# Router columns appended to the expert matrix, taken in pieces of 384, 384 and 264 columns; GpSimd gates the third piece

## The reference, cut to what matters

```python
# layer 0, per batch (8), 128 channels, 2304 pixels
x = x + L0_conv_ref(_gn(x), ...)          # group norm, q/k/v, softmax(q k) v, squeeze-excite
# layer 1, on tokens
t = _to_tokens(x)                          # [8, 2304, 128]
t = t + _L1_attn_ref(_ln_t(t))             # softmax(seq seq^T) seq
t = t + _L1_ffn_ref(_ln_t(t), router_w, router_b, expert_w, expert_b)

def _L1_ffn_ref(x, router_w, router_b, expert_w, expert_b):
    router_probs = softmax(x @ router_w + router_b)        # 8 experts
    top_p, top_i = top_k(router_probs, 2)
    top_p = top_p / sum(top_p)
    expert_out = einsum('bnd,edc->bnec', x, expert_w) + expert_b
    return sum over the 2 chosen experts of top_p * expert_out
```

## Time and profile before

| | |
|---|---|
| Median of 3 runs | 2558.91 us (2558.0 to 2559.78) |
| The profiled execution | 2557.83 us, of which the span of the records is 2556.1 us |
| PE busy | 2501.6 us (98%) |
| PEld busy | 2297.1 us (90%) |
| DVE busy | 2125.3 us (83%) |
| ACT busy | 1774.6 us (69%) |
| POOL busy | 544.6 us (21%) |
| granted TensorE clock | 0.998 of full speed |

### The profile page before, as it was taken

The page is one execution under the profiler, slowest core; times in us unless marked ns, Lnnn a source line. Parts: engine busy times, 40 slices in busy tenths (PEclk is TensorE's granted clock), DMA queues, the critical chain, the costliest instruction groups (busy, mean ns, idle before and its releaser), DMA issues.

```text
span 2556.1 us, 45049 instructions
## 1 busy us (share of the span) xinstructions
PE 2501.6 (98%) x14929; PEld 2297.1 (90%) x14929; DVE 2125.3 (83%) x6242; ACT 1774.6 (69%) x3478; POOL 544.6 (21%) x930
## 2 busy tenths in 40 slices
PE   7999999999999999999999999999999999999998
PEld 5889989899898998999989999899998999989997
DVE  6896888878888788887888878888789887898778
ACT  4667766677667776776767767667676677767775
POOL 0010221112220132111321113111141202312134
PEclk9999999999999999999999999999999999999999
DMA  1000000000000000000000000000000000000000
GB/s 68 10 1 1 4 29 1 23 4 7 26 1 23 4 7 26 23 1 4 10 23 23 1 4 10 23 23 1 4 10 23 23 1 4 23 10 4 1 10 13
DMA packets 13621, 32.53 MB, mean 13 GB/s; under 512 B 1616, under 2 KB 8016, under 8 KB 13392
## 3 DMA queue, kind: packets, MB, share of 16 engines
q1 hardware_dynamic: 13392, 29.64, 3.4%
HBM read 20.20 MB, written 9.44 MB: 12 GB/s over the span
## 4 chain that ended last, share of the span: by engine, by line
PE 74%; DVE 17%; ACT 5%; issue 3%; POOL 0%; DMA 0%; ACTq 0%; DVEq 0%; SPq 0%; POOLq 0%
PE ps L1239 22%; PE ps L1241 21%; PE ps L1240 21%; PE ps L1259 9%; DVE pt_lo L1040 5%; DVE row_space L1025 4%; PE ps L1386 1%; ACT row_space L775 1%; DVE pt_lo L1120 1%; ACT pt_hi L786 1%; ACT row_space L827 1%; DVE pt_lo L1125 1%; DVE gn_raw L898 1%; ACT row_space L872 0%; DVE r L1131 0%
## 5 line engine op out<-in xcount | busy, mean ns | idle before, releaser
L786 ACT ACTIVATE pt_hi<-ps 128x384 fp32r<-128x384 f32 x864 | 415.6, 488 | 301.0 <-PE ps L1259 300.7
L1040 DVE TENSOR_TENSOR pt_lo<-ps,pt_hi 128x384 fp32r<-128x384 f32 x864 | 472.6, 551 | 114.2 <-ACT pt_hi L786 112.2
L1025 DVE TENSOR_SCALAR_CACHE_REDUCE row_space<-ps,key_bias 128x512 f32<-128x512 f32 (+1 forms) x720 | 492.0, 689 | 49.0 <-PE ps L1241 48.1
L775 ACT ACTIVATE row_space<-row_space,negmax 128x512 f32<-128x512 f32 (+2 forms) x432 | 402.8, 932 | 86.0 <-DVE negmax L1034 85.2
L1259 PE MATMUL ps<-ident,row_space 128*128 128x128 f32 x2736 | 444.5, 273 | 5.0 <-ACT row_space L775 3.9
L1259 PEld LDWEIGHTS ps<-ident,row_space 128*128 128x128 f32 x2736 | 345.6, 141 | 76.1 <-ACT row_space L775 7.0
L1239 PE MATMUL ps<-pt_hi,v_hi 128*128 128x384 f32 x864 | 352.4, 408 | 17.2 <-DVE pt_lo L1040 14.9
L827 ACT ACTIVATE row_space<-ps,shift 128x768 f32<-128x768 f32 x260 | 234.1, 900 | 137.4 <-PE ps L1241 132.9
L1125 DVE TENSOR_TENSOR pt_lo<-row_space,pt_hi 128x768 fp32r<-128x768 f32 x260 | 251.3, 967 | 91.6 <-ACT pt_hi L836 91.0
L1239 PE MATMUL ps<-pt_hi,tn_hi 128*128 128x384 f32 x864 | 303.5, 351 | 2.2 <-DVE pt_lo L1125 1.1
L1241 PE MATMUL ps<-pt_hi,v_lo 128*128 128x384 f32 x864 | 292.9, 339 | 0.0
(11 more groups left out here) (229 smaller groups left out, 5396.6 us busy)
## 6 DMA issues: line engine op xcount, KB each, us to landing
x_chan<-x SPq DMA_DIRECT2D x24, 384.0 KB, 4.2
y<-acc SPq DMA_DIRECT2D x48, 192.0 KB, 1.8
t_tok<-tokens SPq DMA_DIRECT2D x8, 768.0 KB, 4.3
t_tok<-tokens SPq DMA_DIRECT2D x8, 384.0 KB, 3.1
t_tok<-eb SPq DMA_DIRECT2D x1, 516.0 KB, 5.4
t_tok<-ew SPq DMA_DIRECT2D x1, 516.0 KB, 6.7
row_space<-wqkv SPq DMA_DIRECT2D x1, 192.0 KB, 3.3
se_sb<-se SPq DMA_DIRECT2D x1, 68.0 KB, 4.1
```

Of the source, the lines that this page charges most:

```text
L775: act.activation(part, part, ACT.Exp, bias=negmax[:, r:r + 1], accum_out=dparts[:, n, r, u:u + 1]).then_inc(p_rows_ready, 1)
L786: act.activation(pt_hi[:, slot, :], ring_bank(step)[:, 0:BW], ACT.Copy)\
L1025: dve.tensor_scalar(row_part(n, r, a, w), ring_bank(step)[:, 0:w], key_bias[:, row:row + 1], None, ALU.add, ALU.max, accum_out=mx[:, row % ...
L1040: dve.tensor_tensor(pt_lo[:, slot, :], ring_bank(step)[:, 0:BW], pt_hi[:, slot, :], ALU.subtract).then_inc(pt_lo_ready, 1)
```

## The change

The 8 router columns join the 1024 expert columns in one matrix of 1032 (`ew_hi`, `ew_lo`). A tile takes it in three pieces. `expert`: 384 columns, experts 0 to 2, gated by VectorE. `scaled`: 384 columns, experts 3 to 5, gated by ScalarE. The new step `mix`: 264 columns, experts 6 and 7 and the logits. The separate router matmuls and the sum of their halves are gone. `mix` comes first for all three tiles of a block; ScalarE copies the 8 logits and then, ungated, the 256 expert columns into SBUF. `router` is VectorE's work alone and waits for the logits of the third tile. GpSimd multiplies the 256 columns by their gates and adds them up with ScalarE's terms in wider additions. `mix` and `router` join `SOON`, so that in the second attention they stand ahead of `p1low`. Most MoE slots are set anew; block 4, the left-over block, has its router no longer in stage 1 but in stage 3 of the next first attention.

```diff
-EARLIER_BLOCK = {1: {8: [('uln',)], 10: [('uapply',)], 13: [('ut',)], 16: [('router',)]}, 2: {1: [('gates',)]},
-                 3: {6: [('expert', 0)], 9: [('scaled', 0)], 12: [('expert', 1)], 13: [('scaled', 1)]},
-                 4: {4: [('expert', 2)], 9: [('scaled', 2)]}}
+EARLIER_BLOCK = {1: {8: [('uln',)], 10: [('uapply',)], 13: [('ut',)]},
+                 3: {3: [('mix', 0)], 4: [('mix', 1)], 5: [('mix', 2), ('router',)], 7: [('gates',)], 10: [('expert', 0)], 13: [('scaled', 0)]},
+                 4: {3: [('expert', 1)], 5: [('scaled', 1)], 8: [('expert', 2)], 10: [('scaled', 2)]}}
...
-MOE_SLOTS = [(6, 9, 11, [13, 13, 15, 16, 17, 18]), (22, 25, 26, [28, 28, 31, 31, 32, 33]), (31, 34, 35,
-             [37, 38, 39, 40, 41, 42]), (39, 42, 43, [45, 45, 46, 46, 47, 47]), (44, 48, 49, [50, 51, 51, 52, 52, 54])]
+MOE_SLOTS = [(6, 9, [10, 11, 11], [13, 13, 15, 16, 17, 18]), (22, 24, [25, 26, 26], [28, 28, 31, 31, 32, 33]),
+             (31, 34, [35, 35, 36], [38, 38, 39, 40, 41, 42]), (39, 42, [43, 43, 44], [46, 46, 47, 48, 49, 49]),
+             (44, 49, [50, 50, 51], [52, 53, 53, 54, 54, 55])]
...
-LAST_MOE_SLOTS = [(6, 9, 11, [13, 13, 15, 16, 17, 18]), (21, 24, 25, [26, 26, 28, 29, 30, 31]), (27, 32, 33,
...
+LAST_MOE_SLOTS = [(6, 9, [10, 11, 11], [13, 13, 15, 16, 17, 18]), (21, 24, [25, 25, 26], [28, 28, 29, 30, 31, 31]),
+                  (27, 32, [33, 33, 34], [35, 36, 36, 37, 38, 39]), (39, 41, [42, 42, 43], [44, 44, 45, 45, 46, 46]),
+                  (43, 47, [48, 48, 49], [50, 50, 51, 51, 52, 52]), (49, 53, [54, 54, 55], [57, 57, 58, 60, 60, 62]),
+                  (56, 59, [60, 61, 61], [63, 63, 64, 64, 65, 65])]
...
-SOON = ("expert", "scaled", "vproj", "qproj", "score", "row_max", "gates")
+SOON = ("mix", "router", "expert", "scaled", "vproj", "qproj", "score", "row_max", "gates")
...
+                elif kind == "mix":
+                    m, k = step[2:]
+                    act.wait_ge(ring_full, filled(step))
+                    if k == 0 and at(gates_ready, "gates", b, m) > 1:
+                        act.wait_ge(gates_ready, at(gates_ready, "gates", b, m) - 1)
+                    act.activation(logits[:, k, :], ring_bank(step)[:, 256:256 + E], ACT.Copy).then_inc(logits_ready, 1)
+                    if mix_block_before(b, m):
+                        act.wait_ge(tile_added, at(tile_added, "scaled", *mix_block_before(b, m), k))
+                    act.activation(mix_pair(m, k), ring_bank(step)[:, 0:256], ACT.Copy).then_inc(mix_terms_ready, 1)
...
                 elif kind == "router":
-                    dve.wait_ge(ring_full, filled(step))
                     shape = [128, TPB, E]
-                    link(dve.tensor_reduce(logits[:, :, :],
-                                           ring_bank(step)[:, 0:TPB * 2 * E].rearrange("p (t h e) -> p t e h", h=2,
-                                                                                       e=E), AX.X, ALU.add))
+                    dve.wait_ge(logits_ready, at(logits_ready, "mix", b, m, TPB - 1))
...
-                elif kind == "router":
-                    for k in range(TPB):
-                        pe.matmul(out, u_low(b, m)[:, tile], rw_pair[:, :, :], start=True, stop=False)
-                        ins = pe.matmul(out, u_high(b, m)[:, tile], rw_pair[:, :, :], start=False, stop=True)
+                elif kind == "mix":
+                    cols = slice(2 * GATED * 128, FOLD)
+                    three(ring_bank(step)[:, 0:256 + E], u_high(b, m)[:, tile], u_low(b, m)[:, tile], ew_hi[:, cols],
+                          ew_lo[:, cols]).then_inc(ring_full, 1)
...
+                    pool.tensor_tensor(tiled(mixed), tiled(mixed), gate, ALU.mult).then_inc(terms_paired, 1)
                     pool.wait_ge(terms_ready, at(terms_ready, *step))
-                    pool.tensor_tensor(term[0], term[0], term[1], ALU.add).then_inc(terms_paired, 1)
-                    pool.tensor_tensor(term[2], term[2], term[3], ALU.add).then_inc(terms_paired, 1)
+                    pool.tensor_tensor(term[:, 0:256], term[:, 0:256], mixed, ALU.add).then_inc(terms_paired, 1)
...
+                    pool.tensor_tensor(term[:, 0:256], term[:, 0:256], term[:, 256:512], ALU.add).then_inc(terms_paired, 1)
+                    pool.tensor_tensor(term[:, 0:128], term[:, 0:128], term[:, 128:256], ALU.add).then_inc(terms_paired, 1)
+                    pool.tensor_tensor(total, total, term[:, 0:128], ALU.add).then_inc(tile_added, 1)
```

More of the change, by code:

```diff
@@ L121, in statistics, with moe @@
                                                   ("se_in", b), ("se_out", b)]
-def moe(b, m, norm, ut, router, experts):
-    s = {router: [("router", b, m)], router + 1: [("gates", b, m)]}
+def moe(b, m, norm, ut, mixes, experts):
+    s = {}
+    for k, slot in enumerate(mixes):
+        s.setdefault(slot, []).append(("mix", b, m, k))
+    merge(s, {mixes[-1]: [("router", b, m)], mixes[-1] + 1: [("gates", b, m)]})
     if ut is not None:
@@ L286 @@
     "ut": ["ring_full", "u_hi_ready", "u_lo_ready"],
-    "router": ["ring_full", "logit_max_ready"], "gates": ["gate_exp_ready", "gates_ready"],
+    "mix": ["ring_full", "logits_ready", "mix_terms_ready"], "router": ["logit_max_ready"], "gates": ["gate_exp_ready", "gates_ready"],
     "expert": ["ring_full", "expert_added"], "scaled": ["ring_full", "terms_ready", "terms_paired", "tile_added"],
@@ L293 @@
         "qproj": "q_lo_ready", "pt": "pt_lo_ready", "ot": "o_added", "tnt": "tnt_lo_ready", "o1t": "o1_added",
-        "ut": "u_lo_ready", "router": "logit_max_ready", "expert": "expert_added", "scaled": "terms_ready"}
-CHAINED = {"stat": 1, "gn_dev": 2, "se_out": 6, "rowsum": 3, "ot": 2, "ln": 6, "o1add": 5, "uln": 6, "router": 8, "gates": 3,
-           "expert": 3, "lnapply": 2, "uapply": 2}
+        "ut": "u_lo_ready", "mix": "mix_terms_ready", "expert": "expert_added", "scaled": "terms_ready"}
+CHAINED = {"stat": 1, "gn_dev": 2, "se_out": 6, "rowsum": 3, "ot": 2, "ln": 6, "o1add": 5, "uln": 6, "router": 7, "gates": 3,
+           "expert": 2, "lnapply": 2, "uapply": 2}
 LAST_BLOCK, LAST_TILE = (B - 1, NB - 1), ("scaled", B - 1, NB - 1, TPB - 1)
 def linked(step):
-    return 4 if step == LAST_TILE else CHAINED.get(step[0], 0)
+    return 5 if step == LAST_TILE else CHAINED.get(step[0], 0)
 def count():
@@ L420, in build @@
         p_rows = row_space[:, 0:5 * NTOK].rearrange("p (s w) -> p s w", s=5)
-        terms = p_rows[:, 2, LW:LW + 2 * 5 * 128].rearrange("p (s a w) -> p s a w", s=2, a=5)
+        terms = p_rows[:, 2, LW:LW + 1024].rearrange("p (s w) -> p s w", s=2)
         keep = sb("keep", [128, TPS - 1, LW])
@@ L640, in _ @@
                 if b + 1 < B:
-                    sp.wait_ge(xg_norm_ready, at(xg_norm_ready, "xgnorm", b, LB - 1))
+                    sp.wait_ge(ring_full, filled(("rows", b, 0)))
                     if b:
@@ L761, in take @@
                     act.wait_ge(bias_folded, 1)
-                    act.activation(rw_pair[:, 0, :], rw_stage, ACT.Copy).then_inc(e_hi_ready, 1)
-                    act.activation(ew_hi[:, :], ew_stage, ACT.Copy).then_inc(e_hi_ready, 1)
+                    act.activation(ew_hi[:, :], fold_w, ACT.Copy).then_inc(e_hi_ready, 1)
                 elif kind == "qproj":
@@ L870, in take @@
                         act.wait_ge(tile_added, at(tile_added, "scaled", *earlier))
-                    for e in range(E // 2):
+                    for e in range(GATED):
                         ins = act.activation(term_of(b, m, k, e), ring_bank(step)[:, e * 128:(e + 1) * 128],
-                                             ACT.Identity, scale=gates[:, m % 2, k, E // 2 + e:E // 2 + e + 1])
+                                             ACT.Identity, scale=gates[:, m % 2, k, GATED + e:GATED + e + 1])
                     ins.then_inc(terms_ready, 1)
@@ L1199, in take @@
                         dve.wait_ge(tile_added, at(tile_added, "scaled", *earlier))
-                    sums = acc[:, m % 2, k, :], term_of(b, m, k, 4)
-                    for e in range(E // 2):
+                    sums = acc[:, m % 2, k, :], term_of(b, m, k, GATED)
+                    for e in range(GATED):
                         term = ring_bank(step)[:, e * 128:(e + 1) * 128]
@@ L1216, in take @@
                     m, k = step[2:]
-                    term = [term_of(b, m, k, i) for i in range(5)]
+                    term = [term_of(b, m, k, i) for i in range(GATED + 1)]
                     total = acc[:, m % 2, k, :]
                     dve.wait_ge(expert_added, at(expert_added, "expert", b, m, k))
-                    link(dve.tensor_tensor(total, total, term[4], ALU.add))
+                    link(dve.tensor_tensor(total, total, term[GATED], ALU.add))
+                    dve.wait_ge(mix_terms_ready, at(mix_terms_ready, "mix", b, m, k))
                     dve.wait_ge(terms_ready, at(terms_ready, *step))
+                    for i in range(2):
```

(8 more changed lines are left out.)

82 lines of the change are left out of this document (47 added, 35 removed).

## The result

The changed kernel takes 2605.2 us (median, 2604.9 to 2606.4) against 2558.7 for the kernel before: ratio 1.0182, 95% interval 1.0170 to 1.0195. It is slower by 46.5 us, where 10 were forecast; 2605 lies outside the range of 2530 to 2588.

The account below looks back on a forecast made before the run. PE, busy 98%, was taken as the bound. Its saved work -29, left-over block -12 and stalls with last batch and tail +51.5 gave +10.5 on 2557.8, 2568; 2569 us as median, range 2530 to 2588.

Parts of the forecast that it names:

- PE's work, -29: PE matmuls: a tile falls from 1.62 to 1.42 us, -29 us over 144 tiles if PE never waits more.
- Rival 2: PE: 16-column matmuls were free, so removing them gives 0 and the third piece costs the savings: 2598 us; chance 0.04.
- VectorE, ScalarE, GpSimd cost nothing by themselves: Whole run: VectorE about 47 us less, ScalarE about 30 more, GpSimd some 120 more, with no cost in time by themselves.
- slot 26: Block 0, second attention: a score waits for mix 1's bank, which ScalarE empties late: 0.9 us a batch.
- Left-over block, -12: Stage 1: PE's wait behind block 4's router goes, 1.7 us seven times, -12 us; stage 3 costs 0.
- Router ahead of `p1low`, 45.5: Seven batches: late `p1low` and banks stall PE, 7 x (3.1 + 1.9 + 0.9) + 6 x 0.7 = 45.5 us.
- slot 10: Mix 0, third behind `qproj` and `vproj`, waits for `q_lo`: 0.7 us, six times.
- slot 46: Block 2: `m1` waits for the low half of slot 44, a stall of 1.9 us a batch.
- `pv1` 36: Block 1: PE waits at `pv1` 36 for `p1low` 36, late behind the router: 0.7 us.
- Last batch and tail, +6: Last batch: router before `p1low` costs 3 us in four blocks; router and gates 4 delay the final chain, +3.
- Rival 1: PE's gain comes through because slack swallows the follow-up stalls: 2541 us, over 2515 to 2555; chance 0.36.
- rival 3: GpSimd's extra 120 us lengthens VectorE operations such as `p1low`: +12 us, 2581 us; chance 0.10.

Follow-up runs that it names:

- 136-column matmuls: Kernel before with pieces of 512, 384 and 136 columns, router columns riding with one expert's so three tiles fit one bank: 2548.2 us, ratio 0.9956.
- three banks alone: Kernel before with each tile's 16-column router matmuls in a ring bank of its own, emptied by ScalarE copies: 2600.3 us, ratio 1.0164.
- block 4 at home: Changed kernel with the left-over block back in its old slots, router at the end of stage 1: 2592.7 us.
- version with two mixes: Changed kernel with all MoE slots as before, router behind `p1low`, third mix of each block left out (tile 2 takes tile 1's results): 2554.1 us.
- version with all at home: Changed kernel with the MoE slots of before in all batches, left-over block included, and router behind `p1low`: 2581.1 us.

## Why the prediction was wrong, point by point

- **PE's work, -29:** right; 2433 to 2404 by distances. Rival 2 is out. The 136-column matmuls are 0.11 us apart as well. The isolated gap of the Trainium skill (TensorE: Matmul & The Clock Gate, Back-to-back issue gap) would be 136/2.4 + 2.5 = 59 ns, an estimate by that page; the trace, in which each matmul has a weight load of its own, disagrees, as it did for 16 columns.
- **VectorE, ScalarE, GpSimd cost nothing by themselves:** GpSimd's multiplication, nearly so (2.3 us, shown); its wider additions were not tested. VectorE has 18 us less to do and not 47; 12 of the 29 are its low halves with both inputs in SBUF, which got longer, from 967 to 994 ns and, where they read `keep`, from 953 to 1029. With three banks alone, where GpSimd has what it had before, they stay at 968 and 953. ScalarE, no. Its copies have the price that I took (0.18 and 0.38), but a bank comes free only when ScalarE's queue gets to them, and that I counted at slot 26 alone.
- **Left-over block, -12: this is the step that failed, with the wrong sign.** The two tables moved in the kernel before cost +12.4, about 8 of it by block 4; in the changed kernel, where `IMAGE` stayed as it was, block 4's place was worth 12.5 and 14.0. I read the wait of stage 1 as the router's because the router stood ahead of it; without it 1.1 us of 1.8 stay. And I gave stage 3 a price of 0, while the router there costs three waits of 1.8 us together: stage 3 had less room than its single slots showed.
- **The group norm steps of `IMAGE`: a term that the prediction does not have,** put at nothing without a reason; about 4 us. With the block this is 24 of the 37 us of the miss. Another 5 in the first attention are work that the new slots leave over for it: 159.7 with block 4 at home, 159.0 with the old slots as well, seven times.
- **Router ahead of `p1low`, 45.5 in the seven batches: size right, cause wrong.** Waits found in a middle batch, with the forecast in brackets: slot 10 0.8 (0.7), slot 26 0.7 (0.9), slot 38 1.4 (1.4), slot 46 1.9 (1.9), 49 0.7 (0.5), 51 0.4 (0.3), expert 1 of block 3 1.0 (0.85). The one at `pv1` 36 did not come (0.7), in its place 0.75 for the low half of u at slot 35. But moving the router behind `p1low` returns 0.4 us, so that the sum came out right is in part luck. The prediction has every link of the chain and names the wrong one as the cause. The new one is that three mixes need three banks of a ring of two. Packed into one slot, the third waits for ScalarE; spread over two, the logits come late. The new slots cost 9.7 us against the old (2590.8 to 2581.1), that is, spreading is the dearer of the two ways.
- **Last batch and tail, +6 without PE's share:** 11.8. The o1 sum behind router 4 and `uln` behind gates 4 came as told (3.4 us more waiting); but the waits ahead of it (2.8 for a `u_tok`, 1.6, 1.3, 1.2) are larger than the 3 us allowed.
- **Rival 1** failed as the waits did not shrink; **rival 3** is 2.3 us for the multiplication, and open for the additions. Its sentence on `p1low` holds for the 342 of 432 that read SBUF alone; the other 90, the one of slot 44 among them, read PSUM and did not get longer.

In a chain of versions: before 2559.3; joined columns and ungated pair in the old slots +21.7; new slots +9.7; block 4 moved +14.0; router ahead of `p1low` +0.4; changed kernel 2605.2. Of the +21.7, the three banks (+40.6 by themselves) and PE's -28.7 make 11.9. Of the other 10, about 4 are the group norm steps, which stay moved in this version: its stages 5 and 6 show the same added waits. But the 40.6 have some 6 us of the lower clock in them, and this version only 1.6. So 6 to 10 us are open. ScalarE's longer copies in the same place are a likely part, but no run has them alone, and waits do not add exactly, as the version with two mixes shows.

## What to carry to other kernels

Count banks before columns: a step that took one buffer of a small ring and now takes three can cost more than it saves (here 40.6 us against 29) when an in-order engine with long work empties them. If the narrow part of a product is to be joined to a wider one, choose a width for which all tiles still fit one bank. A wait that follows a late operation is not caused by it until a run without that operation shows it gone. Slots that look free one by one are not free when the engine behind them has no time to catch up: moving work there can cost more in waits than it saved. And each table that an edit moves needs a term in the sum, even a small one.

## What the runs showed of the hardware

After some of the longer waits PE's granted clock is at the lower of its two levels for a while. Busy time by windows in the changed kernel, after a wait of 2.84 us for `u_tok` that ended at 2530.84 (window and its length; PE, PEld, DVE, ACT, POOL busy; granted clock; DMA share and GB/s):

```profile
2520.00:2530.00 10.00, 8.16 (x49) 7.77 (x48) 8.76 (x27) 7.49 (x11) 8.39 (x11) 1.00 0.03 10
2530.80:2533.70 2.90, 2.86 (x10) 2.86 (x11) 1.41 (x2) 0.58 (x1) 0.00 (x0) 0.51 0.00 0
```

At 0.51, that is 1.2 GHz, matmuls of 384 columns are 0.32 us apart instead of 0.174, about 1.3 us on top of the wait. A wait of 1.3 us at slot 35 was followed by the same in one of seven batches of the version with all at home (0.55 from 931.4 to 935.2, that second attention 1.5 us longer), and one of 2.0 us came with it in two of seven batches of the version with three banks. So a large wait can cost more than its length.
